# First layer: exponentials clamped afterwards, most divisions as an ACT inverse root with one Newton step on DVE; second layer: two PSUM banks swapped and the order at both ends

## The reference

```python
decay = exp(-exp(w)) * (0.5 + 0.5 * tf)            # one number per channel and batch
ek  = exp(minimum(k, 30.0)); ekv = ek * v
nf, df = scan(a = a*decay + ekv), scan(b = b*decay + ek)      # forward in time
nb, db = the same scans, backward
euk = exp(minimum(u + k, 30.0))
num = nf + nb - ekv + euk * v
den = df + db - ek  + euk
base = sigmoid(r) * (num / maximum(den, 1e-08))     # r is x at this layer
cond = base * (0.8 + 0.2 * tf)
```

## Time and profile before

| | us |
|---|---|
| median of 3 runs | 472.86 |
| lowest and highest run | 471.51, 472.87 |
| profiled execution, its own time | 470.68 |
| profiled execution, first to last instruction (span) | 468.9 |
| PE busy | 405.2 |
| DVE busy | 341.3 |
| ACT busy | 235.2 |
| POOL busy | 239.6 |

### The profile page before, as it was taken

How to read it: one execution, slowest core, us unless ns; L and a number is a source line. 1 busy time by engine, 2 the same in 40 slices (tenths; PEclk the granted TensorE clock), 3 DMA queues, 4 the chain that set the end, 5 groups by cost and what they waited for, 6 DMA issues and landing times.

```text
span 468.9 us, 5896 instructions
## 1 busy us (share of the span) xinstructions
PE 405.2 (86%) x1678; PEld 257.2 (55%) x1685; DVE 341.3 (73%) x619; ACT 235.2 (50%) x471; POOL 239.6 (51%) x336
## 2 busy tenths in 40 slices
PE   2577999999999999958784899999999999986794
PEld 1466678755455555625562355556666555653553
DVE  5999887999999999789967367547646511028995
ACT  4600276176667766647886323233233233329884
POOL 6544142578778997224000556775775464214641
PEclk9998999999999999976997799999999999999999
DMA  7900000645565645000011798899899986050001
GB/s 228 398 6 0 1 2 30 228 173 176 189 213 192 218 163 207 18 1 1 2 63 37 247 400 301 287 361 330 290 336 349 309 281 257 24 190 0 13 34 47
DMA packets 23664, 77.39 MB, mean 165 GB/s; under 512 B 3440, under 2 KB 7920, under 8 KB 20176
## 3 DMA queue, kind: packets, MB, share of 16 engines
q1 hardware_dynamic: 20336, 69.94, 41.8%
q0 software_dynamic: 2208, 6.03, 4.0%
q10 hardware_dynamic: 1088, 1.05, 0.7%
HBM read 71.76 MB, written 5.24 MB: 164 GB/s over the span
## 4 chain that ended last, share of the span: by engine, by line
PE 34%; issue 5%; DVE 4%; ACT 4%; DMA 3%; POOL 1%; POOLq 0%; ACTq 0%; DVEq 0%
PE bank L1887 17%; PE bank L1907 10%; PE bank L1898 2%; DVE gl L1495 2%; PE bank L1870 1%; DVE pt L1502 1%; ACT q2T L811 1%; PE bank L1763 1%; PE bank L1744 1%; DMA xb<-cond_rows,row_i 1%; PE bank L1941 1%; DMA gy<-y_rows 1%; DMA cond_rows<-cond 1%; PE bank L1755 1%; POOL st L606 1%
## 5 line engine op out<-in xcount | busy, mean ns | idle before, releaser
L1887 PE MATMUL bank<-gu,xbT 128*128 128x512 f32 x184 | 83.2, 595 | 0.9 <-ACT xbT L876 0.9
L1674 PE MATMUL bank<-hx,w2raw 128*128 128x512 f32 x128 | 67.3, 607 | 4.6 <-DVE hx L1230 3.8
L1431 DVE TENSOR_TENSOR hm<-bank,sl 128x512 f32<-128x512 f32 x23 | 15.9, 692 | 67.2 <-issue 31.1
L756 ACT ACTIVATE rl<-bank 128x512 f32<-128x512 f32 x64 | 38.0, 594 | 40.0 <-PE bank L1538 39.2
L1887 PEld LDWEIGHTS bank<-gu,xbT 128*128 128x128 f32 x184 | 34.5, 190 | 35.6 <-issue 33.3
L542 POOL DMA_INDIRECT xb<-cond_rows,row_i x23 | 26.1, 1133 | 49.9 <-DVE row_i L1381 36.5
L1536 PE MATMUL bank<-xlhi,w1hi 128*128 128x512 f32 x64 | 49.3, 771 | 0.0
L1907 PE MATMUL bank<-dn,hT 128*128 128x256 f32 x184 | 45.2, 388 | 3.4 <-ACT hT L887 0.7
L1230 DVE TENSOR_TENSOR hx<-bank,cwb 128x512 f32<-128x512 f32 x64 | 42.2, 661 | 4.8 <-ACT bank L760 4.7
L467 POOL TENSOR_TENSOR fw<-fw,bw 128x256 f32<-128x256 f32 x32 | 24.0, 750 | 41.8 <-DVE bw L1034 41.4
L549 POOL DMA_INDIRECT y_rows<-yb,dest_i x23 | 25.1, 1089 | 35.5 <-ACT yb L893 34.5
(11 more groups left out here) (294 smaller groups left out, 911.8 us busy)
## 6 DMA issues: line engine op xcount, KB each, us to landing
gu<-in_gu SPq DMA_DIRECT2D x22, 1024.0 KB
cwb<-cw_rows SPq DMA_DIRECT2D x32, 512.0 KB, 4.2
dn<-in_dn SPq DMA_DIRECT2D x23, 512.0 KB, 4.6
traw<-in_t SPq DMA_DIRECT2D x3, 1024.0 KB
w1raw<-in_w SPq DMA_DIRECT2D x8, 256.0 KB, 4.9
w2raw<-in_w SPq DMA_DIRECT2D x8, 256.0 KB, 4.5
kT<-in_kt SPq DMA_DIRECT2D x4, 256.0 KB, 4.9
x<-in_x SPq DMA_DIRECT2D x2, 512.0 KB, 7.0
```

What stands on the lines that cost most here:

```text
L756: act.activation(rl[:, u % 3, :], bank[u % 4][:], ACT.Relu).then_inc(sem("r_ready"), 1)
L1674: pe.matmul(bank[4 + s][:], w2raw[:, e // 4 % 2, e % 4, :], hx[:, 0, u % 4, :], start=(e == 0), stop=(e == E0 - 1), skip_group_check=True) ...
L1887: ins = pe.matmul(bank[2 * (b % 2) + up][:], xbT[:, b % 2, k, :], gu[:, b % RING, k, up * I2:up * I2 + I2], start=(k == 0), stop=(k == KC ...
```

## The change

In the first layer ACT exponentiates k and k + u directly (u as its bias), and DVE clamps the result at e^30 in place. Blocks 0 and 1 keep the DVE reciprocal. For blocks 2 to 7 ACT reads den from PSUM and writes a first inverse (an inverse root, then a square), and DVE makes one Newton step of it: the product with den goes back into PSUM, the step overwrites `euk`, and the gain has the opposite sign, which `make_cond` takes back with a negative factor. Den gets two banks (7 and 5) in turn. POOL computes `ekk * k` of batch 0 as well and splits `sm_raw` in two halves. PE gets matmuls of the identity without a reader (`keep_going`). The exponentials of blocks 8 and 9 are moved behind ACT's work on the shared net. In the second layer `make_cond(1, 3)` reads bank 5 in place of 2, the transposes for it move behind `turn_rows(1)`, and at the end of the layer the last tile's `turn_hidden` stands ahead of `second(6)`, `l1_out(7)` ahead of `make_cond(2, 0)`, and two of the four `turn_gain(2, ...)` behind the loop.

```diff
+E30 = math.exp(30.0)
+DIVIDED = 2
...
-            return bank[((0, 1, 1, 7), (0, 1, 6, 2), (0, 1, 2, 3), (0, 2, 1, 3))[l][b]]
+            return bank[((0, 1, 1, 7), (0, 1, 6, 5), (0, 1, 2, 3), (0, 2, 1, 3))[l][b]]
...
-            return bank[(4, 7)[d]][:, 0:S]
+        def first_num_sum():
+            return bank[4][:, 0:S]
+        def first_den_sum(n):
+            return bank[(7, 5)[n % 2]][:, 0:S]
...
-            return bank[(4, 6, 5, 7)[v]]
+            return bank[(4, 6, 2, 7)[v]]
... (POOL)
-            wkv_kup(NBLK, 1, 0)
-            wkv_kup(NBLK + 1, 2, 0)
+            side_value(0)
             first_value(0)
             first_value(1)
... (ACT)
             def first_exp(n):
-                act.wait_ge(sem("kup_ready"), n + 1)
-                act.activation(first_euk(n), first_euk(n), ACT.Exp).then_inc(sem("eu_ready"), 1)
+                act.activation(first_euk(n), kT[:, n, :], ACT.Exp, bias=ul[:, 0, n % KC:n % KC + 1]).then_inc(sem("eu_raw"), 1)
+            def first_inverse(n):
+                act.wait_ge(sem("sum_den"), n + 1)
+                act.activation(fw[:, n % 2, 1, :], first_den_sum(n), ACT.Abs_reciprocal_sqrt, bias=tiny[:],
+                               scale=2.0 ** -14).then_inc(sem("r0_ready"), 1)
+                act.wait_ge(sem("r0_ready"), 2 * (n - DIVIDED) + 1)
+                act.activation(fw[:, n % 2, 1, :], fw[:, n % 2, 1, :], ACT.Square, scale=2.0 ** -7).then_inc(sem("r0_ready"), 1)
-            wkv_exp(NBLK, 0)
-            wkv_exp(NBLK + 1, 1)
             sigmoid_x(0)
...
+            for n in range(DIVIDED, NBLK):
+                if n == 6:
+                    cond_high(0, (0,))
+                first_inverse(n)
+                if n == DIVIDED:
+                    act.wait_ge(sem("sm_in"), 16)
+                    act.activation(sm_hi[:], sm_raw[:], ACT.Copy).then_inc(sem("sm_high"), 1)
+            load_table(0, ACT.Sigmoid)
...
             load_table(4, ACT.Exp)
+            wkv_exp(NBLK, 0)
+            wkv_exp(NBLK + 1, 1)
...
-            load_table(1, ACT.Gelu_apprx_tanh)
             l1_first(1)
+            load_table(1, ACT.Gelu_apprx_tanh)
... (DVE)
+            def clip_key(b):
+                dve.wait_ge(sem("ek_raw"), b + 1)
+                dve.tensor_scalar(ekk[:, 2 * b:2 * b + 2, 1, :], ekk[:, 2 * b:2 * b + 2, 1, :], E30, None, ALU.min
+                                  ).then_inc(sem("ek_ready"), 1)
+            def clip_bonus(b):
+                dve.wait_ge(sem("eu_raw"), 2 * b + 2)
+                dve.tensor_scalar(GT[:, 1, 2 * b:2 * b + 2, :], GT[:, 1, 2 * b:2 * b + 2, :], E30, None, ALU.min
+                                  ).then_inc(sem("euk_ready"), 1)
...
+            def newton_product(n):
+                dve.wait_ge(sem("r0_ready"), 2 * (n - DIVIDED) + 2)
+                dve.scalar_tensor_tensor(out=first_den_sum(n), in0=fw[:, n % 2, 1, :], scalar=1e8, in1=first_den_sum(n),
+                                         op0=ALU.min, op1=ALU.mult).then_inc(sem("newton"), 1)
+            def newton_step(n):
+                dve.wait_ge(sem("newton"), 2 * (n - DIVIDED) + 1)
+                dve.wait_ge(sem("euv_ready"), n + 1)
+                dve.scalar_tensor_tensor(out=first_euk(n), in0=first_den_sum(n), scalar=2.0, in1=fw[:, n % 2, 1, :],
+                                         op0=ALU.subtract, op1=ALU.mult).then_inc(sem("newton"), 1)
+            def newton_gain(n):
+                dve.wait_ge(sem("sum_num"), n + 1)
+                dve.wait_ge(sem("newton"), 2 * (n - DIVIDED) + 2)
+                dve.scalar_tensor_tensor(out=GT[:, 0, n, :], in0=first_euk(n), scalar=-1e8, in1=first_num_sum(),
+                                         op0=ALU.max, op1=ALU.mult).then_inc(sem("G_ready"), 1)
+            def quotient(n, part):
+                if n < DIVIDED:
+                    step = {2: first_reciprocal, 3: first_gain}.get(part)
+                else:
+                    step = {1: newton_product, 2: newton_step, 3: newton_gain}.get(part)
...
+            between = {(0, 1): [lambda: clip_bonus(0), side_columns], (0, 3): [lambda: clips(1)],
+                       (1, 3): [lambda: clips(2)], (2, 3): [lambda: clips(3)],
...
+            l1_out(NT - 1)
             make_cond(2, 0)
             make_cond(2, 1)
-            l1_out(NT - 1)
... (PE)
+            keep_going(bank[3][:, 0:P], 18, ident[:], ident[:])
             for n in range(6):
                 first_den(n)
+                if n < 5:
+                    keep_going(bank[3][:, 0:P], 2, ident[:], ident[:])
                 first_num(n)
...
             turn_gain(1, 2)
-            turn_gain(1, 3)
...
             turn_rows(1, "", "q1_ready")
-            pe.wait_ge(sem("cond_ready"), 8)
+            turn_gain(1, 3)
+            pe.wait_ge(sem("x1_ready"), 3)
             l1_up(1)
...
                 if t == NT - 2:
                     pe.wait_ge(sem("pre_ready"), NT)
-                    for b in range(B):
-                        turn_gain(2, b)
+                    turn_gain(2, 0)
+                    turn_gain(2, 1)
+                    turn_hidden(NT - 1, "", "q2_ready")
                 second(t, "", "x2_ready", lambda c: q2w[:, c, :])
...
+            turn_gain(2, 2)
+            turn_gain(2, 3)
```

More of the change, by code:

```diff
@@ L12 @@
+import math
 from contextlib import ExitStack
@@ L115, in build @@
         b2bc = sb("b2bc", [P, C])
-        table = sb("table", [P, 7])
+        table = sb("table", [P, 8])
+        tiny = sb("tiny", [P, 1])
         te = sb("te", [P, B, 64])
@@ L471, in wkv_sums, with split_side @@
                     pool.tensor_tensor(fw[:, p, d, :], fw[:, p, d, :], eu[:, p, d, :], ALU.add).then_inc(sem("sum_" + part), 1)
-            pool.wait_ge(sem("kup_ready"), 1)
-            wkv_kup(NBLK, 1, 0)
-            wkv_kup(NBLK + 1, 2, 0)
+            def split_side(k):
+                pool.wait_ge(sem("sm_high"), 1)
+                pool.tensor_tensor(sm_lo[:, k, :], sm_raw[:, k, :], sm_hi[:, k, :].bitcast(F32), ALU.subtract).then_inc(sem("sm_low"), 1)
+            side_value(0)
             first_value(0)
             first_value(1)
-            for b in range(1, B):
-                side_value(b)
-            route_consts()
-            for n in range(2, NBLK):
-                first_value(n)
-                if n == 3:
-                    pool.wait_ge(sem("sm_high"), 1)
-                    pool.tensor_tensor(sm_lo[:], sm_raw[:], sm_hi[:].bitcast(F32), ALU.subtract).then_inc(sem("sm_low"), 1)
+            side_value(1)
+            first_value(2)
+            side_value(2)
+            first_value(3)
+            split_side(0)
+            side_value(3)
+            first_value(4)
+            split_side(1)
+            first_value(5)
+            route_consts()
+            first_value(6)
+            pool.wait_ge(sem("te_sum"), 2)
+            wkv_kup(NBLK, 1, 0)
+            first_value(7)
+            wkv_kup(NBLK + 1, 2, 0)
             def split_w1(eg):
@@ L741, in _ @@
             shared_first(0)
-            load_table(0, ACT.Sigmoid)
             scores_copy(E0, bank[4], 1, 1)
@@ L1103, in _ @@
             dve.wait_ge(sem("consts"), 4)
-            first_kup(0)
-            first_kup(1)
-            for part in range(2):
-                wkv_scan(0, 0, 0, 0, part)
-            side_next(1)
-            side_value_0()
+            clip_key(0)
             for n in range(NBLK):
                 for part in range(4):
-                    if n or part >= 2:
-                        wkv_scan(n, 0, n, n % 2, part)
-                    if n and part == 2:
-                        first_reciprocal(n - 1)
-                    if n and part == 3:
-                        first_gain(n - 1)
+                    wkv_scan(n, 0, n, n % 2, part)
+                    quotient(n - 1, part)
                     for step in between.get((n, part), ()):
                         step()
+            newton_product(NBLK - 1)
+            newton_step(NBLK - 1)
             make_cond(0, 2)
-            first_reciprocal(NBLK - 1)
-            first_gain(NBLK - 1)
+            newton_gain(NBLK - 1)
             def weight_max(m):
@@ L1566, in cT, with keep_going @@
                 return cThi[:, k, a:b], cTlo[:, k, a:b]
+            def keep_going(out, n, lhs, rhs):
+                for i in range(n):
+                    pe.matmul(out, lhs, rhs, start=True, stop=True)
             pe.wait_ge(sem("ident_ready"), 1)
@@ L1614, in first_add @@
                 pe.wait_ge(sem("scan_" + part), n + 1)
-                wait(pe, sem("G_ready" if d == 0 else "rden_ready"), n)
-                pe.matmul(first_sum(d), ident[:], fw[:, n % 2, d, :], start=True, stop=False)
-                pe.matmul(first_sum(d), ident[:], bw[:, n % 2, d, :], start=False, stop=False)
-                pe.wait_ge(sem("euv_ready" if d == 0 else "eu_ready"), n + 1)
-                pe.matmul(first_sum(d), ident[:], last, start=False, stop=True).then_inc(sem("sum_" + part), 1)
```

(17 more changed lines are left out.)

88 lines of the change are left out of this document (39 added, 49 removed).

## The result

| | before | changed |
|---|---|---|
| median, us | 472.87 (471.51 to 473.18, 4 runs) | 461.47 (459.93 to 462.28, 4 runs) |
| profiled execution, its own time | 470.68 | 462.28 |
| its span | 468.9 | 460.5 |

The ratio is 0.9767 with a 95% interval of 0.974 to 0.9794, 9.7 to 12.3 us of 472.87; the ratio itself stands for 11.0.

The account below looks back on a forecast made before the run. The prediction took DVE to bound the first layer's scans and PE what follows. First layer -7.0, clock +0.7, second layer -2.0 and +0.3 sum to -8.0 us: 472.86 becomes 464.9, range 461.0 to 469.0.

Parts of the forecast that it names:

- rival 3: More comes out: no clock spell, no waits of the small operations, room for the scans; 462.1 us, chance 0.1.
- block 3's first scan: First layer's start: new order of preparation and clamps brings block 3 to 22.5 from 25.31 us, -2.8.
- from there to block 7: First layer, Newton blocks: two operations at 0.43 us replace a reciprocal of 1.65, -0.79 per block, four blocks.
- from there to the scores: End of first layer: PE's scores start at 44.2 instead of 51.21 us, making the layer's sum -7.0.
- clock spell in the first layer: Idle gaps of PE in blocks 1 and 2 bring one spell at the low clock level, +0.7 us.
- start of the second layer: With bank 5, DVE no longer waits 1.99 us for PE's second-tile matmuls after `make_cond(1, 3)`, -2.0 us.
- rest of it, to `make_cond(2, 0)`: End of the second layer: new order puts `make_cond(2, 0)` at 242.4 instead of 242.16, +0.3 us (0 to 0.5).
- Clamps that lose to POOL: First-layer scans: each pair's second clamp waits for POOL's product, three pairs cost 3.0 us; 467.9, chance 0.15.
- Second layer gives nothing: What follows in the second layer waits for POOL or ACT anyway; 466.9 us, chance 0.08.
- PE at its low clock through the stage: First-layer scans: low clock costs +2.36 us in each of five blocks, 11.8 in all; 476.0, chance 0.06.
- Nothing that counts: DVE's gain is taken by PE's order or ACT's latency; time within 0.3% of before, chance 0.03.

Follow-up runs that it names:

- small_first: Changed kernel with the four small operations placed ahead of the clamp of `euk` instead of behind it; 460.85 us, one run.
- divided8: Changed kernel with the DVE reciprocal in all eight blocks, no inverse root and no Newton step; 466.52 us, ratio 0.9882.
- no_fill: Changed kernel without the first layer's matmuls without a reader; 459.67 us, ratio 0.9745.
- second_only: Kernel before with the edits of the second layer alone; 470.81 us, ratio 0.9964.
- first_only: Changed kernel with all edits of the second layer taken back; 463.43 us, ratio 0.9816.
- before_cover13: Kernel before with 13 instead of 9 matmuls without a reader ahead of the third layer's first gathered block; 471.90 us, ratio 0.9992.
- best_b: Changed kernel with the edits of no_fill, cover13, small_first and gather_free; 460.31 us, ratio 0.9765.
- best_a: Changed kernel with the edits of no_fill, cover13 and small_first; 458.94 us, ratio 0.9718.
- gather_free: Changed kernel with the first half of block 1's up weights loaded behind the third layer's first gather, not ahead; 460.32 us, ratio 0.9760.
- cover13: Changed kernel with 13 instead of 9 matmuls without a reader ahead of the third layer's first gathered block; 459.82 us, ratio 0.9734.

## Why the prediction was right, and where its sizes were off

**The direction, the mechanism and the range held, the range by 0.5 us.** The forecast was 464.9 (461.0 to 469.0), the measured median 461.47. It is the case of rival 3, more comes out, which had a chance of 0.1. That the median lies inside the range is in part luck: with the 12.62 us of the layers alone it would have been 460.3, and what was given back in the third layer, which I had not seen, brought it in. By the prediction's own steps, in the changed kernel's trace:

| step | forecast, us | measured, us |
|---|---|---|
| block 3's first scan | 22.5, -2.8 | 20.98, -4.33 |
| from there to block 7 | -3.2 | 36.97, -3.80 |
| from there to the scores | -1.0 | 41.69, -1.39 |
| clock spell in the first layer | +0.7 | none |
| scores to `make_cond(1, 2)` | 0 | -0.76 |
| start of the second layer | -2.0 | -2.07 |
| rest of it, to `make_cond(2, 0)` | +0.3 | -0.27 |
| sum there | -8.0 | -12.62 |
| gather, transposes and block 0 | 0 | +4.3 in this execution |

**The start was mis-sized by 1.5 us.** I charged 0.6 for the clamp of `euk`, 0.7 for the small operations and 1.1 for two waits of them; the rows give 0.35 (7.95 to 8.30) and 0.99 (8.30 to 9.29) with one wait of 0.55. Blocks 1 and 2 took 4.93 instead of 5.13. The mechanism of the wait was right, and small_first shows it, but the first three operations took their usual 0.16 to 0.18, though the third started 0.03 behind POOL's product; only the fourth waited.

**The Newton block.** I priced its two operations by the gain's 0.43 from start to start; they take 0.32 (3.43 a block against my 3.59). The same gain ahead of a clamp takes 0.31, so some 0.12 of the 0.43 come with the next block's scan and not with the operation. divided8 confirms the whole: 4.9 us, where 5 x 0.79 and some tenths for the last block would have been 4.2.

**The clock charge of +0.7 was wrong.** I read the lower level in the kernel before as a sign that idle gaps in blocks 1 and 2 bring it about. The additions stay 0.43 apart and the granted clock reads 1.00 up to 43.9, with idle gaps of 1.17 us in both of these blocks; in no_fill, with gaps of 1.41 and 1.61, they stay 0.43 apart too. Nor had that spell cost anything before: second_only, the same up to there, has none from 42 to 66 (1.00 instead of 0.93), though PE idled 1.88 us ahead of 43.3 there as in the kernel before (1.87), and starts its scores at 51.19, against 51.21. What brought the spell about is open.

**The second layer** was priced rightly at its start. The order at its end costs 0.05, not 0.3: from `l1_pre(1)` to `make_cond(2, 0)` the kernels with the old order take 33.92 at the least (first_only, before_cover13) and those with the new one 33.97 (second_only, best_b). The stretch varies from one execution to the next, up to 35.05 in best_a and 34.26 in the kernel before, so the -0.27 above is no effect of the change. Nor is most of the -0.76 ahead of it: from the scores to `make_cond(1, 2)` the eleven traces with the first layer's change have 152.4 to 153.1 us, the three without 152.8 to 153.4.

**What I left out** is the last row. I took it that a gain made up to 242 reaches the end. Nearly all of it does, but the third layer starts on a race between the gather, the weights and PE's clock: the gather took 3.80 in the kernel before and 4.08 to 5.24 in eight kernels that have the first layer's change and weights ahead of it, the cause being the weights (gather_free). With the clock this gives back up to 4.3 us; cover13 seems to win some 1.7 of it back, though the intervals overlap. The two errors have opposite signs: the layers brought 4.6 more than I said, and of these the medians keep 3.0 to 3.4. Why the gather lands later after the change is open: second_only too had 4.34, the kernel before 3.80 with the same weights ahead of it, and in every trace where they are ahead the last of these weights starts 2.2 us before the gather, so it is not their distance.

**The rivals.** Clamps that lose to POOL (0.15): not as placed, by 0.17 us; placed one scan later they cost 2.8 us, near the 3.0 that I had put on it. Second layer gives nothing (0.08): out. PE at its low clock through the stage (0.06): out, even without the matmuls meant to prevent it. Nothing that counts (0.03): out.

## What to carry to other kernels

Where a DVE operation and one of POOL's keep each other off, who starts first decides: put a short DVE operation of this kind directly behind the one whose semaphore releases POOL, not a scan later. Splitting a long division into an activation on an idle engine and two short operations pays where the dividing engine is the full one; price the short ones from start to start, not by their own length, and from a row that has the same kind of operation behind it (0.31 and 0.43 for the same gain). And when a stage is shortened, look at the first transfer and the first matmuls of the next stage that no earlier work covers: here, with four more matmuls without a reader, the clock held through block 0 and the time was some 1.7 us lower, and moving a transfer out of the way made another one late.
